# Cross attention: subtractions and row maxima in two halves of two PSUM banks, direct scores for two row groups at a time

## The reference

```
q = layernorm(x) @ Wq + bq          # 16 sequences, 64 queries, 16 heads of 16 channels
k = ctx @ Wk + bk ; v = ctx @ Wv + bv   # 1601 keys for each sequence, 192 channels in
scores  = q k^T / sqrt(16)
weights = softmax(scores over the 1601 keys)
x = x + (weights v) @ Wo + bo
```

## Time and profile before

| what | us |
|---|---|
| median of 3 runs (2981.04, 2987.51, 2992.98) | 2987.51 |
| the profiled execution's own time | 2980.99 |
| its span, first to last instruction | 2979.3 |
| TensorE busy in the whole span | 2530.0 (85%) |
| VectorE busy in the whole span | 1785.9 (60%) |
| ScalarE busy in the whole span | 1074.4 (36%) |

### The profile page before, as it was taken

How to read it: one execution, slowest core, us unless ns; L and a number is a source line. 1 busy time by engine, 2 the same in 40 slices (tenths; PEclk the granted TensorE clock), 3 DMA queues, 4 the chain that set the end, 5 groups by cost and what they waited for, 6 DMA issues and landing times. The chain is left out here.

```text
span 2979.3 us, 79011 instructions
## 1 busy us (share of the span) xinstructions
PE 2530.0 (85%) x35280; PEld 1835.2 (62%) x35280; DVE 1785.9 (60%) x2577; ACT 1074.4 (36%) x1606; POOL 753.6 (25%) x964
## 2 busy tenths in 40 slices
PE   5898988889879799888888869875988899988598
PEld 2555555556555455455555545533888889988487
DVE  4665656566553444499999958248566665564500
ACT  2444444444442111355555531234333333332111
POOL 6910000000000000033323340030666655663200
PEclk9999999999987699899999979888999999998699
DMA  2101010000000011322323210000000000000131
GB/s 73 39 21 39 21 39 21 24 36 21 21 8 16 11 37 37 80 81 73 96 67 84 68 49 0 0 28 7 4 4 4 3 4 4 4 4 3 57 141 43
DMA packets 23576, 101.89 MB, mean 34 GB/s; under 512 B 4824, under 2 KB 9837, under 8 KB 16494
## 3 DMA queue, kind: packets, MB, share of 16 engines
q1 hardware_dynamic: 23278, 97.31, 10.1%
HBM read 96.25 MB, written 1.05 MB: 33 GB/s over the span
## 5 line engine op out<-in xcount | busy, mean ns | idle before, releaser
L609 DVE TENSOR_TENSOR xa_probT<-psum,xa_minus_max_spread 128x2048 f32<-128x2048 f32 (+1 forms) x112 | 239.6, 2139 | 162.0 <-PE psum L353 161.5
L592 DVE TENSOR_REDUCE xa_minus_max_parts<-psum 128x4 f32<-128x1600 f32 (+1 forms) x128 | 233.9, 1827 | 165.5 <-PE psum L334 165.5
L522 ACT ACTIVATE xa_probT<-xa_probT,zero_column 128x2048 f32<-128x2048 f32 (+1 forms) x112 | 210.6, 1880 | 271.4 <-DVE xa_probT L609 271.3
L1264 POOL TENSOR_TENSOR tk_exp_all<-tk_exp_all,tk_exp_left 128x577 f32<-128x577 f32 x64 | 121.0, 1890 | 354.2 <-ACT tk_exp_left L1385 354.2
L2002 POOL TENSOR_TENSOR pa_cT<-pa_mt_and_qw,pa_levelT 128x256 f32<-128x256 f32 x256 | 192.5, 785 | 64.2 <-PE psum L2036 64.2
L2174 ACT ACTIVATE pa_x<-psum 128x256 f32<-128x256 f32 x256 | 98.4, 384 | 304.1 <-PE psum L2036 291.2
L2250 DVE TENSOR_TENSOR pa_inv_and_invT<-pa_inv_and_invT,psum 128x512 f32<-128x512 f32 x192 | 132.1, 688 | 121.6 <-PE psum L2036 121.6
L701 POOL MEMSET la_v<- 128x512 f32 x1 | 0.5, 526 | 730.3 <-remote 730.3
L324 PE MATMUL psum<-xa_wv,xa_ctxT 64*128 64x256 f32 x1248 | 179.5, 395 | 3.3 <-ACT xa_v L515 2.2
L334 PE MATMUL psum<-xa_kT,xa_qb 32*128 32x400 f32 (+1 forms) x1024 | 125.4, 559 | 66.4 <-DVE xa_probT L609 45.2
L2036 PE MATMUL psum<-pa_inv_and_invT,pa_cT 64*64 64x64 f32 x4096 | 151.3, 235 | 33.7 <-DVE pa_prob L2211 30.1
(11 more groups left out here) (471 smaller groups left out, 5040.7 us busy)
## 6 DMA issues: line engine op xcount, KB each, us to landing
xa_ctxT<-in_xa_ctx SPq DMA_DIRECT2D x16, 1344.0 KB, 5.7
tk_ctx<-in_ctx SPq DMA_DIRECT2D x16, 1248.0 KB, 5.4
tk_ctxT<-in_ctxT SPq DMA_DIRECT2D x16, 1200.8 KB
ec_w<-in_ec_w SPq DMA_DIRECT2D x16, 1024.0 KB, 6.8
m_gate_up<-in_m_gate_up SPq DMA_DIRECT2D x17, 256.0 KB, 2.6
m_down<-in_m_down SPq DMA_DIRECT2D x17, 128.0 KB, 2.5
ff_w<-in_ff_w SPq DMA_DIRECT2D x2, 1024.0 KB
x_resident<-in_x SPq DMA_DIRECT2D x1, 1024.0 KB, 4.8
```

The source lines that it names most:

```text
L522: a_(o, o, ACT.Exp, bias=core.zero[0:w]).then_inc(e_done, 1)
L592: v_.tensor_reduce(part[:, :, n // 4, n // 2 % 2 + 2 * (n % 2)], ps[:, 0:4, 0:z - a], AX.X, ALU.max, negate=True).then_inc(m_used, 1)
L609: v_.tensor_tensor(o[:, :, 0:chunks], got[:, :, 0:chunks], shift[0:w, h].rearrange("p j r n -> p (j r) n").unsqueeze(2).broadcast_to([w, 8 ...
```

## The change

A subtraction is now two instructions, over banks 0 and 1 and then over banks 2 and 3 (1024 values each), and each signals `sub_done`. A reduction is now two as well (800 values each), each with its own wait for the direct scores of its two banks, and each signals `m_used`. `direct` does the matmuls of row groups 0 and 1 behind a wait for the first half, and those of row groups 2 and 3 behind a wait for the second half; each pair signals `m_ps`. All counts that others wait for are doubled: `scores`, the exponentials and `maximum` still wait for both halves. The number of matmuls and what they compute are the same.

```diff
@@ -326,11 +326,17 @@
                 if 2 in thirds and i in (1, 3, 5, 6):
                     mm.then_inc(v_ps, 1)
 
-            def direct(b, h, n):
+            def direct(b, h, n, freed):
 
                 r, (a, z) = n // 4, PARTS[n // 2 % 2 + 2 * (n % 2)]
                 pe.wait_ge(k_sb, 4 * b + n // 2 + 1)
-                for j in range(4):
+                for p, (sem_, count) in enumerate(freed):
+                    pe.wait_ge(sem_, count)
+                    direct_pair(h, r, a, z, p)
+
+            def direct_pair(h, r, a, z, p):
+
+                for j in (2 * p, 2 * p + 1):
                     mm = mmul(ps[:, j, 0:z - a], qb[quad[j], h, r, :, :].rearrange("p e t -> p (e t)"),
                               kT[quad[j], h, r, a:z], start=True, stop=True)
                 mm.then_inc(m_ps, 1)
@@ -415,8 +421,7 @@
                     project(y)
 
             def last_maximum(b, h, y):
-                pe.wait_ge(m_used, MAXES * b + 7)
-                direct(b, h, 7)
+                direct(b, h, 7, [(m_used, 2 * (MAXES * b + 6) + p + 1) for p in range(2)])
                 if b + 1 < B:
                     pe.wait_ge(ctx_loaded[1 - h], 16 * ((b + 1) // 2) + 16)
                     pe.wait_ge(v_sb, 4 * b + 4)
@@ -434,21 +439,20 @@
             for t in range(ROUNDS):
                 under_shift(0, 0, t)
                 if t == 0:
-                    pe.wait_ge(qb_ready, 1)
+                    direct(0, 0, t, [(qb_ready, 1), (qb_ready, 1)])
                 else:
-                    pe.wait_ge(m_used, t)
-                direct(0, 0, t)
+                    direct(0, 0, t, [(m_used, 2 * t - 1), (m_used, 2 * t)])
                 under_maximum(0, 0, t, False, None)
             last_maximum(0, 0, None)
 
             def body(n, i, h, first, last):
                 for t in range(ROUNDS):
                     if t:
-                        pe.wait_ge(sub_done, 7 * n + t)
+                        pe.wait_ge(sub_done, 2 * (7 * n + t))
                     if not last:
-                        pe.wait_ge(m_used, MAXES * (n + 1) + t)
+                        pe.wait_ge(m_used, 2 * (MAXES * (n + 1) + t))
                     if t == 0 and last:
-                        pe.wait_ge(m_used, MAXES * (n + 1))
+                        pe.wait_ge(m_used, 2 * MAXES * (n + 1))
                     scores(n, h, t)
                     if t == 0:
                         if not first:
@@ -470,8 +474,7 @@
                         continue
                     y = None if first or h else i - 1
                     under_shift(n + 1, 1 - h, t)
-                    pe.wait_ge(sub_done, 7 * n + t + 1)
-                    direct(n + 1, 1 - h, t)
+                    direct(n + 1, 1 - h, t, [(sub_done, 2 * (7 * n + t) + p + 1) for p in range(2)])
                     under_maximum(n + 1, 1 - h, t, not first, y)
                 if not last:
                     last_maximum(n + 1, 1 - h, y)
@@ -516,7 +519,7 @@
 
             def exponentials(n, h, t):
                 w = width(2 * t)
-                act.wait_ge(sub_done, 7 * n + t + 1)
+                act.wait_ge(sub_done, 2 * (7 * n + t + 1))
                 o = probT[0:w, (7 * h + t) % 2].rearrange("p j r c n -> p (j r) c n")
                 o = o.rearrange("p u c n -> p (u c n)") if t < 6 else o[:, :, 0, :]
                 a_(o, o, ACT.Exp, bias=core.zero[0:w]).then_inc(e_done, 1)
@@ -588,12 +591,14 @@
 
             def reduce(b, n):
                 a, z = PARTS[n // 2 % 2 + 2 * (n % 2)]
-                dve.wait_ge(m_ps, MAXES * b + n + 1)
-                v_.tensor_reduce(part[:, :, n // 4, n // 2 % 2 + 2 * (n % 2)], ps[:, 0:4, 0:z - a], AX.X, ALU.max,
-                                 negate=True).then_inc(m_used, 1)
+                for p in range(2):
+                    two = slice(2 * p, 2 * p + 2)
+                    dve.wait_ge(m_ps, 2 * (MAXES * b + n) + p + 1)
+                    v_.tensor_reduce(part[:, two, n // 4, n // 2 % 2 + 2 * (n % 2)], ps[:, two, 0:z - a], AX.X, ALU.max,
+                                     negate=True).then_inc(m_used, 1)
 
             def maximum(b, r):
-                dve.wait_ge(m_used, MAXES * b + 4 * r + 4)
+                dve.wait_ge(m_used, 2 * (MAXES * b + 4 * r + 4))
                 v_.tensor_reduce(nmax[:, r], part[:, :, r], AX.X, ALU.min).then_inc(max_step, 1)
 
             def subtract(n, h, t, first):
@@ -604,10 +609,13 @@
                     dve.wait_ge(n_sb, 2 * n + 2)
                 if not first or t >= 2:
                     dve.wait_ge(pv_done, 7 * n + t - 1)
-                got = ps[0:w, 0:4, :].rearrange("p j (r c n) -> p (j r) c n", r=2, c=2)
-                o = probT[0:w, (7 * h + t) % 2].rearrange("p j r c n -> p (j r) c n")
-                v_.tensor_tensor(o[:, :, 0:chunks], got[:, :, 0:chunks],
-                                 shift[0:w, h].rearrange("p j r n -> p (j r) n").unsqueeze(2).broadcast_to([w, 8, chunks, P]), ALU.add).then_inc(sub_done, 1)
+                for p in range(2):
+                    two = slice(2 * p, 2 * p + 2)
+                    got = ps[0:w, two, :].rearrange("p j (r c n) -> p (j r) c n", r=2, c=2)
+                    o = probT[0:w, (7 * h + t) % 2, two].rearrange("p j r c n -> p (j r) c n")
+                    v_.tensor_tensor(o[:, :, 0:chunks], got[:, :, 0:chunks],
+                                     shift[0:w, h, two].rearrange("p j r n -> p (j r) n").unsqueeze(2).broadcast_to(
+                                         [w, 4, chunks, P]), ALU.add).then_inc(sub_done, 1)
 
             def normalise(b):
                 dve.wait_ge(t_ps, b + 1)
```

## The result

| | us |
|---|---|
| before, median of 4 runs (2980.52 to 2992.98) | 2984.28 |
| changed, median of 4 runs (2943.51 to 2958.37) | 2954.53 |
| ratio, 95% interval | 0.9898 [0.9874, 0.9921] |
| changed, profiled execution, its span | 2951.78, 2950.1 |

The change makes the kernel about 1% faster, 30 us by these medians. Two later measurements of the same kernel gave 0.991 [0.9891, 0.993] and 0.9941 [0.9921, 0.9961], with medians of 2954.07 and 2955.52 for it and of 2977.47 and 2975.96 for the kernel before.

What follows compares the result with a forecast made beforehand. TensorE was taken as nearly the bound, busy 89.64 of 100 us, its idle tenth recoverable. Terms of -12.3 us plus -6 for the clock gave -18, so 2969.5, stated as 2970 us; range 2957 to 2994.

Steps and rivals of the forecast that it cites:

- t = 1: Round with keys ending in `turn_out`: TensorE free for the scores slightly earlier, gain 0.05 us a batch.
- last batch end: Before the last batch no keys follow, so the maximum being ready earlier counts in full: gain 0.7 us.
- the base: Time of the unchanged kernel from which the gain was subtracted: 2987.5 us as a median, 2981.0 profiled.
- t = 0 and 2: Rounds with keys: early first pair lets reduction and scores start sooner, gain 0.5 us each, 1.0 in a batch.
- t = 3 to 5: Rounds with values: the later second half delays the work behind it, loss 0.07 us each, 0.2 a batch.
- batch ends 0 to 13 at full clock: Last direct scores' second pair starts later and the next keys stand behind it: loss 0.07 us a batch.
- places at 0.50 (ends 0 to 13): Batch ends at 1.2 GHz: less idle TensorE removes about half of 8 counted, -6 us, bounds 0 and -13.
- last batch, opening and tail: Last batch has seven subtractions chained with its scores, +0.5 us; opening held up by ScalarE's copies, 0.
- Price of halves: On VectorE, two half subtractions end 0.07 us later than one whole, bounds 0.0 and 0.15; two half reductions take 1.90.
- Pairs of row groups: Direct scores on TensorE: a pair alone takes 0.89 us, and the second pair fully overlaps a first one halfway.
- the third rival: Pairs start in strict order on TensorE, second one pass (0.44 us) behind: +10 us, 2985 or 2979; chance 0.08.
- the keys hide that: At the batch end the maximum is ready 0.7 us earlier, but the next keys (2.29 us) cover it: no gain.

Runs made afterwards that it cites:

- the late last direct scores: Changed kernel, but the last direct scores of a batch wait for both halves of the reduction before the first pair: 2966.54 us, ratio 0.9952.

## Why the prediction was wrong, point by point

The direction, the mechanism and the places were right. Two steps failed. The sum of the gain was too small: its charges for the later second halves, +3.0 us for the rounds with values and +1.0 for the batch ends, measured +0.7 and -0.6, and what it gave to t = 1 and to the last batch end, -1.2 and -0.7, measured -2.4 and -2.6. And the base, 2987.5 us, was too high by some 10. Both columns are for the first pair of profiles, us over the whole layer:

| term | predicted | measured |
|---|---|---|
| t = 0 and 2 | -15 | -15.2 |
| t = 1 | -1.2 | -2.4 |
| t = 3 to 5 | +3.0 | +0.7 |
| batch ends 0 to 13 at full clock | +1.0 | -0.6 |
| last batch end | -0.7 | -2.6 |
| places at 0.50 (ends 0 to 13) | -6 | -6.1 |
| last batch, opening and tail | +0.5 | +2.4 |
| sum, cross attention | -18.4 | -23.8 |

The last row before the sum is chance: in the second pair of profiles it is -2.0 instead of +2.4, the last batch end is -0.9, and the layer gains 26.6.

**Price of halves: right.** 2.35 to 2.36 and 1.89 us; the second half starts 0.08 early.

**Pairs of row groups: right.** Full overlap, shown by the run with one pair behind the other. Strict order, the third rival, did not show: where both pairs are free (round 6, 326.84 to 327.73) the direct scores take 0.89 as before; all four first passes start from 326.84 to 326.86, and the second passes 0.44 later. This is the place where the Trainium skill, "TensorE: Matmul & The Clock Gate", section "Step-by-step: what each phase is for", has matmuls in program order; this trace does not agree, by the same 0.89.

**Rounds t = 0 and t = 2: right**, 6.07 and 6.06 against 6.07.

**Round t = 1 and the value rounds: mis-sized.** In the keys rounds I let a matmul start 0.07 before the modelled end of the one in front, but for `turn_out` I took the modelled end itself (303.37), so the slack was 0.19 and not 0.12: gain 0.13 instead of 0.05. For t = 3 to 5 I charged 0.07 everywhere. It is 0.05 at t = 3, at t = 4 and at t = 5 with `project`, the later second half less 0.02 that the direct scores are shorter; and without `project`, in 8 of 15 batches, the round before had ended with the reduction and not with TensorE's work, so that it gains 0.12. I had sorted t = 5 with the others without reading its rows for both kinds of batch.

**Batch end: "the keys hide that" was wrong.** In the kernel before, `spread_maximum` came 2.31 us behind the keys' start (390.44 to 392.75), now 2.23 (330.64 to 332.87): the maximum had still been the later one, by 0.08. And a half reduction starts 0.99 behind its pair where the whole one started 1.02 behind all four, so the last direct scores came 0.02 later and not 0.07. That turned my +0.07 into -0.05. At the last batch end the 0.7 us were right: TensorE's wait there fell from 2.2 to 1.5 us, before in the first row and changed in the second:

```profile
PE psum L342 <- DVE xa_minus_max L597: 2.2, 1, 2.2
PE psum L348 <- DVE xa_minus_max L602: 1.5, 1, 1.5
```

**The clock: right in kind, the count by luck.** Idle time at the batch end does bring places at 0.50, shown by the late last direct scores: 10 of 14 against 2 or 3. That about half of them would go was a choice between bounds, worked out from no row, and with one pair behind the other ten are there without that idle time. Among the first 14 ends the count fell from 6 to 2. The 8 I had counted take in the last end, which was at 0.50 in both profiles of the kernel before and in the changed kernel's first was not; that is most of its 2.6 us, where I had priced only the 0.7 of the wait.

**The base: the larger half of the miss.** 2970 stood on the 2987.51 of three runs. The later medians of the kernel before are 2984.28, 2977.47, 2980.74 and 2975.96, those of the changed one 2954.53, 2954.07 and 2955.52. From 2978 my 18 us would have led to 2960: of the 15.5 us between 2970 and the measured 2954.5 the base makes some 9.5 and the layer's gain, 23.8 instead of 18.4, makes 5.4. Some 25 us are the gain in the layer; my range's lower end allowed for 30 from that base but took the base for certain.

## What to carry to other kernels

When two engines take turns on the same banks, splitting both engines' turns pays: here -25 us. Splitting the first engine's turn alone filled the other's gap and won nothing (+11 us). Splitting the second's alone gave +7, but that run says less: its late direct scores (0.09 us in each of 90 rounds) and late subtractions (0.06) come from where its waits stand and make some 13 us by my estimate, so without them it may have won the 6 us that I had expected; no run has it so. Where the first engine is then fully busy, the price of the split (0.07 us) turns up in every round that it already ruled. Before summing, sort every kind of round by what ends last in it, with the start-to-start times of rows rather than their modelled ends.

## What the runs showed of the hardware that I had not expected

- The order of two waits in front of one matmul counts: with the late one first, TensorE starts 0.05 to 0.06 us after the subtraction's end, with the late one second 0.15, shown in both directions. The wait written last is an instruction of its own of 51 ns. Over the rounds of the kernel before that is 0.09 us each.
- With the same instructions the linear attention took 119.5, 130.8 and 139.1 us in the three profiles shown, with mean granted clocks of 0.81, 0.72 and 0.67.
- A VectorE instruction that signals by 2 instead of 1 has its last wait as an instruction of its own in front of it and starts 0.03 to 0.09 us later behind TensorE: in three programs, and in one of them again in a second execution. That the signal by 2 is the reason is shown by the kernel before with nothing else edited, in one profile.
